# A spectral convolution and a box filter on one core: one DMA fewer per row on SyncE, and seven row additions moved from GpSimd to VectorE

## The chip, the core and the metric

The kernel runs on one NeuronCore of one Trainium2 chip. The metric is the device time of one launch, in microseconds (us). Every engine follows an instruction stream of its own: TensorE (PE in the profile, PEld for its weight loads), VectorE (DVE), ScalarE (ACT), GpSimd (POOL), and SyncE (SP), which here only issues DMA transfers. They meet at semaphores.

## The reference, cut to what matters

The input x is 8 images of 16 channels, 512 x 512, float32. Two layers follow each other, each with a residual:

```python
# _gn: group norm, 8 groups of two channels, over rows and columns
# layer 0
X = rfftn(_gn(x), axes=(-2, -1)); Xr, Xi = real(X), imag(X)
Yr = rconv(Xr, wr) - rconv(Xi, wi) + b_real      # 3x3 convolutions over the spectrum, 16 -> 16 channels
Yi = rconv(Xr, wi) + rconv(Xi, wr) + b_imag
x = x + irfftn(Yr + 1j * Yi)
# layer 1: mean over a 15 x 15 window, zero padding
x = x + mean_filter(_gn(x), 15)
```

## The kernel before

**No transform is computed.** A 3x3 convolution over a spectrum is, back in the image, a sum of products of the image with slow waves. Layer 0 therefore needs, for each image row, the normalised row, its Hilbert transform along the width, and channel mixing by matrices that depend on the row (base, cosine and sine terms), and a few border ("wrap", "virtual") terms.

**Layout.** The 512 image rows are split into 8 bands of T = 64 rows. A partition holds one channel of one band, so "row t" below is 128 partitions x 512 columns, and an image has 64 of them. The image stays in SBUF (`img`).

**Layer 0, one row** (`layer0` on each engine, `slot` functions). The work is a chain over the engines:
- ScalarE normalises the row into a high float16 part and a float32 copy (`normalise`, L773 and L774); GpSimd subtracts the two for the low part (`split_g`, L1303).
- SyncE turns the row by two DMA transposes (`turn`, L396) into one of two buffers `xT`, after it has waited for the split (L391) and for the Hilbert product of the row two before (L394).
- TensorE multiplies it with the Hilbert matrix (`front_hilbert`, L472, 12 matmuls), ScalarE and VectorE split the product in two parts (L781, L1121), and TensorE mixes channels (`mix`, L562, with the wrap terms at L569, 10 steps of four matmuls in quadrants) into the banks p0, p1, p2. TensorE's order is: Hilbert product of row t+1, then mixing of row t. The late half of a row's p0 terms is done in the mixing of the next row, which then counts `p0_ready`.
- VectorE multiplies p1 and p2 with the waves (`wave_terms`, L1163 and L1169), GpSimd adds these and the image row (`add_terms`, L1310 and L1313), VectorE adds p0 and takes statistics (`finish_row`, L1178 and L1181), ScalarE adds a half mean (L790, L800) and counts the row in `x1_whole`.
- From the third step of a mixing on, TensorE waits until VectorE is through with the p1 and p2 of the row before (L630, L631).

**The matrices.** A row's twelve block matrices (high and low parts of six) are built once in setup by VectorE (L1001), stored to a DRAM tensor `bd_dram` (L376), and fetched for every row of every image into one of RB = 4 slots of `bd_all` (`fetch`, L385). The wrap matrix of a row comes from a table in DRAM into `wrap_mat` (L386). Slot t % 4 is free when row t-4 has been mixed. SyncE's queue is strictly in order; its order is written out in `matrices`: turn row t, wait for row t-4, fetch row t.

**Sums for layer 1.** The box filter needs the sum of rows 0 to 7 (`head`) and of rows 57 to 63 (`tail`). Both are running additions by GpSimd (`presum`, L1324 and L1327), a row at a time, in the slot five rows after the row; `presummed` counts the two finished sums, and ScalarE (L870) and VectorE (L1238) wait for both before layer 1. To hold these additions, GpSimd's first 16 slots are written out, and its loop covers the rest.

**Layer 1** turns rows on TensorE, sums them with a band matrix and stores them; VectorE, ScalarE and GpSimd split and subtract rows, while ScalarE's queue loads the next image. An image is one turn of a hardware loop on every engine; the last image is written out after the loop.

**Setup.** SyncE's queue carries, in this order: 19 tables (L334), the weights and biases (L339 to L344), the first image (L348), and later the matrices' stores. VectorE's long chain begins at L929, when the last weight load has landed.

Of the kernel before, what the change touches and what calls it, by code (L numbers as in the profile page):

```python
# [32 lines left out]
F16 = mybir.dt.float16  # L33
ALU = mybir.AluOpType
ACT = mybir.ActivationFunctionType

P = 128
B, C, H, W = 8, 16, 512, 512
HB = P // C
HL = HB // 2  # L40
# [28 lines left out]
GROUP_T = 4  # L69
REC = 12 * HP  # L70
WRAP_SCALE = 4096.0
# [85 lines left out]
def build(nc, x, w_real, w_imag, b_real, b_imag, tab, bd_dram, out):  # L157
    x_v = x.rearrange("b c (s hl t) w -> b s c hl (t w)", s=2, hl=HL)
    out_v = out.rearrange("b c (s hl t) w -> b s c hl (t w)", s=2, hl=HL)
    with ExitStack() as ctx:  # L160
# [30 lines left out]
        stage = [ob_all[:, s * 3 * W:(s + 1) * 3 * W].bitcast(F16) for s in range(2)]  # L191
        assert GROUP_T * REC <= 6 * W
        vbase, vrow, vterm = q_row[0], q_row[1], term_row[0]
        hv = [sb(f"hv{l}", [NV, 2, HZ], F16) for l in range(2)]
        bd_all = sb("bd_all", [P, RB, REC], F16)
        bd = [bd_all[:, s].rearrange("p (j m) -> p j m", j=12) for s in range(RB)]
        flat_bd = bd_all[:].rearrange("p s r -> p (s r)").bitcast(F32)
# [7 lines left out]
        xT = [row.bitcast(F16).rearrange("p (k m) -> p k m", k=8) for row in (piece[9], xT_more[:])]  # L205
        wrap_mat = [sb(f"wrap_mat{s}", [P, P], F16) for s in range(RB)]
        wrap_row = sb("wrap_row", [P, W], F16)
# [45 lines left out]
        vg_split, vh_split, uv_kept, vz_split = sem("vg_split"), sem("vh_split"), sem("uv_kept"), sem("vz_split")  # L253
        bd_made = sem("bd_made")
        bd_stored = [sem(f"bd_stored{s}") for s in range(2)]
        bd_in = [sem(f"bd_in{s}") for s in range(RB)]
# [74 lines left out]
        def _(sp):  # L331
            for n in TABLES:
                if n not in IN_DRAM:
                    sp.dma_start(tb[n][:], tab[n]).then_inc(tab_in, 16)  # L334
            sp.wait_ge(zeroed, 1)
            for i, wr in enumerate((w_real, w_imag)):
# [37 lines left out]
            for g in range(T // GROUP_T):  # L374
                sp.wait_ge(bd_made, g + 1)
                sp.dma_start(bd_dram[g * GROUP_T:(g + 1) * GROUP_T].rearrange("t p r -> p t r"),  # L376
                             stage[g % 2][:, 0:GROUP_T * REC].rearrange("p (t r) -> p t r", t=GROUP_T)
                             ).then_inc(bd_stored[g % 2], 16)
            for s in range(2):
                sp.wait_ge(bd_stored[s], 8 * (T // GROUP_T))  # L380
            sp.dma_start(tail, tab["hilbert_kernel"]).then_inc(bias_in, 16)

            def matrices(b):
                def fetch(t, s):
                    sp.dma_start(bd_all[:, s], bd_dram[t]).then_inc(bd_in[s], 16)  # L385
                    sp.dma_start(wrap_mat[s][:], tab["wrap_h16"][t]).then_inc(bd_in[s], 16)  # L386

                def turn(t, s, first):

                    sp.wait_ge(g_split, b * T + t + (PRIMED + 1))  # L390
                    sp.sem_inc(split_seen, 1)  # L391
                    if first * NG + s >= 2:
                        sp.wait_ge(h_made, b * T + t + (PRIMED - 1))
                        sp.sem_inc(slot_seen, 1)  # L394
                    for i in range(2):
                        sp.dma_start_transpose(xT[s % 2][:, :, (1 - i) * HP:(2 - i) * HP],  # L396
                                               gp_flat[s][i * HP:(i + 1) * HP]).then_inc(xt_in[s % 2], 16)

                sp.wait_ge(uv_summed, PRIMED + (b + 1) * NCH)
                for t in range(RB):  # L400
                    fetch(t, t)
                for t in range(NG):
                    turn(t, t, 0)
                    if t >= RB:
                        sp.wait_ge(p0_ready, b * T + (PRIMED + t - RB + 1))
                        fetch(t, t % RB)
                with sp.Fori(1, T // NG) as i:
                    for s in range(NG):
                        turn(i * NG + s, s, 1)
                        sp.wait_ge(p0_ready, b * T + i * NG + (PRIMED + s - RB + 1))  # L410
                        fetch(i * NG + s, s % RB)

# [18 lines left out]
        def _(pe):  # L431
# [99 lines left out]
            def layer0(b):  # L531
# [53 lines left out]
                def mix(i, s, first):  # L585
# [34 lines left out]

                    pe.wait_ge(bd_in[s % RB], 32 * (b * (T // RB) + i * (NG // RB) + s // RB + 1))
                    pe.wait_ge(h_split, PRIMED + n + 1)
# [285 lines left out]
        def _(dve):  # L908
# [88 lines left out]
            for g in range(T // GROUP_T):  # L997
                if g >= 2:
                    dve.wait_ge(bd_stored[g % 2], 16 * (g // 2))
                rows = slice(g * GROUP_T, (g + 1) * GROUP_T)  # L1000
                V.tensor_tensor(stage[g % 2][:, 0:GROUP_T * REC].rearrange("p (q c h) -> p q c h", c=C, h=HL),  # L1001
                                smat[:, rows].rearrange("p t j o -> p (t j) o").unsqueeze(3)
                                .broadcast_to([P, 12 * GROUP_T, C, HL]),
                                tb["hl_mask16"][:].unsqueeze(1).unsqueeze(1).broadcast_to([P, 12 * GROUP_T, C, HL]),
                                ALU.mult).then_inc(bd_made, 1)
                for t in itertools.islice(rest, 3):
                    count_row(0, t)
# [82 lines left out]
            def layer0(b):  # L1090
# [92 lines left out]
                def slot(i, s, first):  # L1183
# [6 lines left out]
                    if t + 1 < T:  # L1190
                        low_hilbert(n + 1, (s + 1) % NG)

                slot(0, 0, 0)
                virtual_means()
# [4 lines left out]
                for s in range(NG):  # L1199
                    slot(1, s, 1)  # L1200
                with dve.Fori(2, T // NG - 1) as i:
                    for s in range(NG):
                        slot(i, s, 2)
# [68 lines left out]
        def _(pool):  # L1272
# [26 lines left out]
            def layer0(b):  # L1299
# [15 lines left out]
                def presum(n, t):  # L1315

                    total, links = (head, head_chain) if t <= R else (tail, tail_chain)
                    at_r, start = (t, 0) if t <= R else (t - (T - R), T - R)
                    pool.wait_ge(x1_whole, n + 1)
                    if at_r == 0:  # L1320
                        return
                    rows = R if t <= R else R - 1
                    if at_r == 1:
                        ins = G.tensor_tensor(total, img[:, start, :], img[:, t, :], ALU.add)  # L1324
                    else:
                        pool.wait_ge(links, b * (rows - 1) + at_r - 1)
                        ins = G.tensor_tensor(total, total, img[:, t, :], ALU.add)  # L1327
                    ins.then_inc(links if at_r < rows else presummed, 1)

# [12 lines left out]
                for t in range(1, 3):  # L1342
                    split_g(b * T + t, t)
                for t in range(R + 9):
                    slot(t // NG, t % NG, t // NG, sum_t=t - 5 if 5 <= t <= R + 5 else None)
                assert (R + 9) % NG == 0
                with pool.Fori((R + 9) // NG, T // NG - 1) as i:
                    for s in range(NG):
                        slot(i, s, 2)
                for t in range(T - NG, T):  # L1350
# [54 lines left out]
```

## Time and profile before

| | |
|---|---|
| median of 3 runs | 3860.23 us (3859.74 to 3861.21) |
| the profiled execution's own time | 3868.96 us |
| its span, first to last instruction | 3867.2 us |
| granted TensorE clock, mean | 0.961 |
| busy: TensorE / VectorE / GpSimd / ScalarE | 3360.8 / 3155.5 / 2632.0 / 2109.3 us |
| one image, both layers, about | 463 us, of it 262 us from the first to the last Hilbert product of layer 0 |

Times inside the profile are microseconds from the span's start. A line such as "L562" is a line of the kernel. The chain of waits is followed back from the last instruction, at each step to what released it. "Idle before" is time that the engine stood still ahead of an instruction, with the one that ended it. A large busy share does not make an engine the bound: what counts is which wait ends last in a stage.

### The profile page before, as it was taken

How to read it: one execution, taken by the hardware profiler on the slowest of the kernel's cores; microseconds unless marked ns; L12 is line 12 of the kernel's file. 1: busy time of each engine (PE TensorE's matmuls, PEld its weight loads, DVE VectorE, ACT ScalarE, POOL GpSimd, SP SyncE). 2: the span in 40 equal slices, each digit the busy share in tenths (PEclk: the TensorE clock that was granted, in tenths of full speed). 3: DMA queues.
4: the chain of work that ended last, by engine and by line, in shares of the span. 5: the costliest groups of instructions: out<-in, count | busy, mean ns of one | idle time of the engine just before them, and what ended most of it. 6: DMA issues, size and time to landing. Idle time of an engine off the chain costs nothing.

```text
span 3867.2 us, 115816 instructions
## 1 busy us (share of the span) xinstructions
PE 3360.8 (87%) x38496; PEld 2224.2 (58%) x38496; DVE 3155.5 (82%) x5870; ACT 2109.3 (55%) x4286; POOL 2632.0 (68%) x2177
## 2 busy tenths in 40 slices
PE   2189889997999979899798998999899998999978
PEld 1055576555765557555675556755476555765557
DVE  7888877887778878788787887888877887888976
ACT  0068733786337852578426873278633785247842
POOL 5079853997539966499546985389853996639954
PEclk8599999999999999999999999999999999999999
DMA  6556567554766538655485554755467653865634
GB/s 158 180 100 121 104 176 196 110 121 80 221 170 117 120 83 245 144 118 121 116 235 113 121 118 139 223 108 121 96 185 192 113 121 76 232 162 118 123 79 137
DMA packets 785608, 542.37 MB, mean 140 GB/s; under 512 B 655216, under 2 KB 730576, under 8 KB 772944
## 3 DMA queue, kind: packets, MB, share of 16 engines
q1 hardware_dynamic: 762832, 420.23, 47.9%
q10 hardware_dynamic: 22400, 117.46, 11.6%
q8 instruction: 195, 3.19, 0.4%
q14 instruction: 181, 1.48, 0.1%
HBM read 256.31 MB, written 146.80 MB: 104 GB/s over the span
## 4 chain that ended last, share of the span: by engine, by line
SPq 39%; PE 31%; issue 11%; DVE 11%; ACT 3%; POOL 3%; DMA 2%; ACTq 1%; DVEq 0%; POOLq 0%
SPq L396 27%; PE h_ps L674 14%; PE p L700 6%; SPq L385 5%; PE p L511 4%; SPq L386 4%; DVE ob_all L1235 2%; PE p L562 2%; ACT arena L743 2%; PE p L480 1%; DVE ob_all L1001 1%; ACTq L883 1%; DVE stat L990 1%; PE h_ps L472 1%; DMA xT_more<-arena 1%
## 5 line engine op out<-in xcount | busy, mean ns | idle before, releaser
L562 PE MATMUL p<-arena,bd_all 64*64 64x512 f16 x16896 | 1278.8, 380 | 25.6 <-DVE ob_all L1169 23.7
L1362 POOL TENSOR_TENSOR arena<-img 128x512 f32<-128x512 f32 x392 | 498.7, 1273 | 461.8 <-PE h_ps L674 439.8
L1310 POOL TENSOR_TENSOR ob_all<-ob_all,img 128x512 f32<-128x512 f32 x512 | 662.6, 1294 | 176.2 <-DVE ob_all L1163 169.4
L743 ACT ACTIVATE arena<-h_ps 128x512 f16<-128x512 f32 x512 | 305.7, 597 | 838.2 <-PE h_ps L674 595.0
L562 PEld LDWEIGHTS p<-arena,bd_all 64*64 64x64 f16 x16896 | 562.9, 105 | 347.5 <-issue 139.4
L1313 POOL TENSOR_TENSOR ob_all<-ob_all 128x512 f32<-128x512 f32 x512 | 653.0, 1275 | 40.2
L1163 DVE SCALAR_TENSOR_TENSOR ob_all<-p,bias_c,cosw 128x256 f32<-128x256 f32 x1024 | 448.1, 479 | 167.6 <-PE p L562 138.7
L674 PE MATMUL h_ps<-bd_all,arena 128*128 128x128 f32 x3584 | 539.6, 286 | 0.0
L1219 DVE TENSOR_TENSOR arena<-h_ps,arena 128x512 f16<-128x512 f32 x512 | 353.2, 690 | 207.9 <-ACT arena L743 206.3
L674 PEld LDWEIGHTS h_ps<-bd_all,arena 128*128 128x128 f32 x3584 | 447.6, 191 | 121.2 <-issue 114.7
L800 ACT ACTIVATE img<-img,half_row (+1 forms) x1024 | 484.9, 527 | 4.8
L773 ACT ACTIVATE arena<-img,sc 128x512 f16 (+1 forms) x512 | 432.0, 844 | 32.3 <-POOL arena L1303 31.3
L1169 DVE SCALAR_TENSOR_TENSOR ob_all<-p,bias_c,cosw 128x256 f32<-128x256 f32 x1024 | 443.6, 475 | 0.0
L472 PE MATMUL h_ps<-hilbert,arena 128*128 128x256 f16 x3072 | 379.6, 273 | 63.9 <-DMA arena<-arena 59.3
L472 PE MATMUL h_odd<-hilbert,xT_more 128*128 128x256 f16 x3072 | 380.2, 274 | 58.4 <-DMA xT_more<-arena 45.6
L1303 POOL TENSOR_TENSOR arena<-arena 128x512 f16<-128x512 f32 x256 | 296.9, 1160 | 193.5 <-ACT arena L774 193.5
L472 PEld LDWEIGHTS h_odd<-hilbert,xT_more 128*128 128x128 f16 x3072 | 280.1, 98 | 208.1 <-DMA xT_more<-arena 126.2
L472 PEld LDWEIGHTS h_ps<-hilbert,arena 128*128 128x128 f16 x3072 | 280.0, 98 | 208.1 <-DMA arena<-arena 115.9
L1181 DVE BATCH_NORM_STATS2 stat<-img (+1 forms) x512 | 355.5, 694 | 51.8
L700 PE MATMUL p<-band,arena 128*128 128x135 f16 (+1 forms) x4096 | 332.5, 225 | 58.1 <-DVE ob_all L1235 56.2
L511 PE MATMUL p<-img,bd_all 128*64 128x256 f32 x2048 | 306.5, 406 | 76.0 <-POOL bd_all L1282 49.9
L1235 DVE SCALAR_TENSOR_TENSOR ob_all<-p,img 128x512 f32<-128x512 f32 x512 | 348.7, 681 | 5.1 <-PE p L700 4.3
(166 smaller groups left out, 4992.8 us busy)
## 6 DMA issues: line engine op xcount, KB each, us to landing
out<-ob_all SPq DMA_DIRECT2D x512, 256.0 KB, 4.2
bd_all<-bd_dram SPq DMA_DIRECT2D x512, 192.0 KB, 2.3
img<-in_x ACTq DMA_DIRECT2D x168, 512.0 KB, 7.0
img<-in_x ACTq DMA_DIRECT2D x112, 256.0 KB, 4.9
wrap_mat<-tab_wrap_h SPq DMA_DIRECT2D x512, 32.0 KB, 2.0
img<-in_x SPq DMA_DIRECT2D x24, 512.0 KB, 23.7
bd_dram<-ob_all SPq DMA_DIRECT2D x16, 768.0 KB, 3.5
arena<-arena SPq DMA_TRANSPOSE x512, 2.7
```

Of the source, the lines that this page charges most:

```text
L396: sp.dma_start_transpose(xT[s % 2][:, :, (1 - i) * HP:(2 - i) * HP], gp_flat[s][i * HP:(i + 1) * HP]).then_inc(xt_in[s % 2], 16)
L472: m = mm(dst(a), row[:, 4 * lx + k, :], tb["hilbert16"][:, lt, k, 0:cols], start=(half == 0 and i == 0), stop=(half == 1 and i == 2))
L511: m = mm(uv_ps[i * HP:(i + 1) * HP, cols], w, img[:, 2 * q + i, cols], start=(q == 0 and part == 0), stop=(q == T // 2 - 1 and part == 1), ...
L562: m = mm(bank[out_half * HP:(out_half + 1) * HP, :], bd[s % RB][rows, 6 * lm + (j if own else j + 1), :], part, start=opens and i3 == 0, s ...
L674: m = mm(turned_ps[u % 2][:, k, :], row[:, k * P:(k + 1) * P], mat, start=(i == 0), stop=(i == len(terms) - 1))
L700: m = mm(p0[0][:, lo:hi], parts[u % 2][:, l, k, :], tb["band16"][:, lo - k * P + R:hi - k * P + R], start=(u == 0 and k == 0 and l == 0), ...
L800: ins = nc.scalar.activation(row, row, ACT.Identity, bias=half_row[:, s, a:a + 1])
L1163: ins = V.scalar_tensor_tensor(t1[:, a, :], p1[:, a * HALF:(a + 1) * HALF], bias_c[:, 1, t, 1 - a:2 - a], cosw[:, a, :], ALU.subtract, ALU ...
L1169: ins = V.scalar_tensor_tensor(t2[:, a, :], p2[:, a * HALF:(a + 1) * HALF], bias_c[:, 0, t, 1 - a:2 - a], sinw[:, a, :], ALU.add, ALU.mult)
L1310: G.tensor_tensor(q, term_row[s % 2][0], parity(img[:, t, :]), ALU.add).then_inc(first_added, 1)
L1313: G.tensor_tensor(q, q, term_row[s % 2][1], ALU.add).then_inc(q_done, 1)
L1362: G.tensor_tensor(diff[u % 2], img[:, u + R, :], img[:, u - R - 1, :], ALU.subtract).then_inc(moved, 1)
```

## The change

1. The record of a row in `bd_dram` and `bd_all` grows by 128 elements per partition, which hold the wrap matrix. A DMA from DRAM to DRAM writes the table into the records once, in setup, ahead of the weight loads. The separate fetch L386 is gone, `bd_in` counts 16 per row in place of 32.
2. SyncE's order in layer 0 is: turn row t, wait for row t-5, fetch row t-1; the last row's fetch follows the loop.
3. The head sum (rows 0 to 7) is made by VectorE, behind its other work in slots 9 to 15, instead of GpSimd in slots 6 to 12; GpSimd keeps the tail sum, and its loop begins at row 8.

```diff
-REC = 12 * HP
+REC = 12 * HP + P
...
+        STAGED = 12 * HP
...
-        bd = [bd_all[:, s].rearrange("p (j m) -> p j m", j=12) for s in range(RB)]
+        bd = [bd_all[:, s, 0:STAGED].rearrange("p (j m) -> p j m", j=12) for s in range(RB)]
+        wrap_mat = [bd_all[:, s, STAGED:REC] for s in range(RB)]
...
-        wrap_mat = [sb(f"wrap_mat{s}", [P, P], F16) for s in range(RB)]
...
                     sp.dma_start(tb[n][:], tab[n]).then_inc(tab_in, 16)
+            sp.dma_start(bd_dram[:, :, STAGED:REC], tab["wrap_h16"]).then_inc(wrap_stored, 16)
             sp.wait_ge(zeroed, 1)
...
+            sp.wait_ge(wrap_stored, 16)
             sp.dma_start(tail, tab["hilbert_kernel"]).then_inc(bias_in, 16)
...
                     sp.dma_start(bd_all[:, s], bd_dram[t]).then_inc(bd_in[s], 16)
-                    sp.dma_start(wrap_mat[s][:], tab["wrap_h16"][t]).then_inc(bd_in[s], 16)
...
                 for t in range(NG):
                     turn(t, t, 0)
-                    if t >= RB:
-                        sp.wait_ge(p0_ready, b * T + (PRIMED + t - RB + 1))
-                        fetch(t, t % RB)
+                    if t > RB:
+                        sp.wait_ge(p0_ready, b * T + (PRIMED + t - RB))
+                        fetch(t - 1, (t - 1) % RB)
                 with sp.Fori(1, T // NG) as i:
                     for s in range(NG):
                         turn(i * NG + s, s, 1)
-                        sp.wait_ge(p0_ready, b * T + i * NG + (PRIMED + s - RB + 1))
-                        fetch(i * NG + s, s % RB)
+                        sp.wait_ge(p0_ready, b * T + i * NG + (PRIMED + s - RB))
+                        fetch(i * NG + s - 1, (s - 1) % RB)
+                sp.wait_ge(p0_ready, (b + 1) * T + (PRIMED - RB))
+                fetch(T - 1, (T - 1) % RB)
...
-                    pe.wait_ge(bd_in[s % RB], 32 * (b * (T // RB) + i * (NG // RB) + s // RB + 1))
+                    pe.wait_ge(bd_in[s % RB], 16 * (b * (T // RB) + i * (NG // RB) + s // RB + 1))
...
+                def sum_head(t):
+
+                    dve.wait_ge(x1_whole, b * T + t + 1)
+                    if t == 1:
+                        ins = V.tensor_tensor(head, img[:, 0, :], img[:, 1, :], ALU.add)
+                    else:
+                        dve.wait_ge(head_chain, b * (R - 1) + t - 1)
+                        ins = V.tensor_tensor(head, head, img[:, t, :], ALU.add)
+                    ins.then_inc(head_chain if t < R else presummed, 1)
...
                 for s in range(NG):
                     slot(1, s, 1)
+                    if s > 0:
+                        sum_head(s)
...
-                for t in range(R + 9):
-                    slot(t // NG, t % NG, t // NG, sum_t=t - 5 if 5 <= t <= R + 5 else None)
-                assert (R + 9) % NG == 0
-                with pool.Fori((R + 9) // NG, T // NG - 1) as i:
+                for s in range(NG):
+                    slot(0, s, 0)
+                with pool.Fori(1, T // NG - 1) as i:
                     for s in range(NG):
-                        slot(i, s, 2)
+                        slot(i, s, 1)
```

GpSimd's `presum` keeps only its branch for the tail.

## Rows read from the trace of the kernel before

**Rows 1.** The page of the kernel before: busy shares, queue q1, chain by line, one DMA issue

```profile
PE 3360.8 (87%) x38496; PEld 2224.2 (58%) x38496; DVE 3155.5 (82%) x5870; ACT 2109.3 (55%) x4286; POOL 2632.0 (68%) x2177
...
q1 hardware_dynamic: 762832, 420.23, 47.9%
...
SPq L396 27%; PE h_ps L674 14%; PE p L700 6%; SPq L385 5%; PE p L511 4%; SPq L386 4%; DVE ob_all L1235 2%; PE p L562 2%; ACT arena L743 2%; PE p L480 1%; DVE ob_all L1001 1%; ACTq L883 1%; DVE stat L990 1%; PE h_ps L472 1%; DMA xT_more<-arena 1%
...
bd_all<-bd_dram SPq DMA_DIRECT2D x512, 192.0 KB, 2.3
```

**Rows 2.** SyncE's queue in the steady part of layer 0: start us, us, what

```profile
2197.66 2.52 SPq L396 DMA_TRANSPOSE arena<-arena  x2
2200.37 0.43 SPq L385 DMA_DIRECT2D bd_all<-bd_dram  x1
2200.98 0.33 SPq L386 DMA_DIRECT2D wrap_mat<-tab_wrap_h  x1
2201.65 2.52 SPq L396 DMA_TRANSPOSE xT_more<-arena  x2
```

**Rows 3.** TensorE's timeline: first and ninth Hilbert product, fifth image, then the last

```profile
2173.05 1.48 PE L472 MATMUL h_odd<-hilbert,xT_more 128*128 128x256 f16 x12
...
2205.67 1.48 PE L472 MATMUL h_odd<-hilbert,xT_more 128*128 128x256 f16 x12
...
3548.28 1.48 PE L472 MATMUL h_ps<-hilbert,arena 128*128 128x256 f16 x12 [0.62 <-DMA arena<-arena]
...
3580.27 1.48 PE L472 MATMUL h_ps<-hilbert,arena 128*128 128x256 f16 x12 [0.59 <-DMA arena<-arena]
```

**Rows 4.** TensorE's timeline, fifth image: the Hilbert products of rows 7, 8 and 16

```profile
2088.53 1.48 PE L472 MATMUL h_odd<-hilbert,xT_more 128*128 128x256 f16 x12
...
2092.36 1.48 PE L472 MATMUL h_ps<-hilbert,arena 128*128 128x256 f16 x12
...
2128.57 1.48 PE L472 MATMUL h_ps<-hilbert,arena 128*128 128x256 f16 x12 [0.85 <-DMA arena<-arena]
```

**Rows 5.** Busy us by window: PE, PEld, DVE, ACT, POOL; clock; DMA share; GB/s

```profile
2173.21:2238.38 65.17, 62.23 (x834) 35.78 (x833) 57.65 (x113) 52.78 (x113) 59.00 (x49) 1.00 0.59 121
```

**Rows 6.** VectorE's timeline, rows at TensorE's pace

```profile
2084.58 0.88 DVE L1163 SCALAR_TENSOR_TENSOR ob_all<-p,bias_c,cosw 128x256 f32<-128x256 f32 x2 [0.19 <-PE p L562]
```

**Rows 7.** Timeline of VectorE and GpSimd in one steady row

```profile
2202.70 1.30 POOL L1310 TENSOR_TENSOR ob_all<-ob_all,img 128x512 f32<-128x512 f32 x1 [0.22 <-DVE ob_all L1163]
...
2204.07 1.28 POOL L1313 TENSOR_TENSOR ob_all<-ob_all 128x512 f32<-128x512 f32 x1
...
2204.71 0.67 DVE L1121 SCALAR_TENSOR_TENSOR arena<-h_ps,arena 128x512 f16<-128x512 f32 x1
...
2205.31 1.16 POOL L1303 TENSOR_TENSOR arena<-g_more,arena 128x512 f16<-128x512 f32 x1
```

**Rows 8.** Who waited for whom, the last rows of the second image's layer 0

```profile
PE h_ps L472 <- DMA arena<-arena: 2.5, 2, 1.4
...
PE h_odd L472 <- DMA xT_more<-arena: 1.1, 1, 1.1
```

**Rows 9.** One line, GpSimd's L1327: durations ns min/median/max, first and last start

```profile
L1327 POOL TENSOR_TENSOR arena<-arena,img x88: 1259/1272/1292, 244.6 to 3724.2; 128x512 f32<-128x512 f32 x88
```

**Rows 10.** One line, VectorE's L1114: durations ns min/median/max, first and last start

```profile
L1114 DVE TENSOR_TENSOR ob_all<-ob_all x8: 691/692/692, 207.5 to 3447.2; 128x512 f32<-128x512 f32 x8
```

**Rows 11.** Timeline of setup, VectorE and GpSimd

```profile
24.11 1.23 DVE L320 TENSOR_TENSOR img<-img,trig_h 128x1024 f32<-128x1024 f32 x1
...
31.88 3.33 POOL L321 TENSOR_TENSOR img<-img 128x1024 f32<-128x1024 f32 x1
...
33.03 3.26 DVE L320 TENSOR_TENSOR img<-img,trig_swapped 128x1024 f32<-128x1024 f32 x1
```

**Rows 12.** The start of setup: timeline, then busy time by window (columns as in rows 5)

```profile
17.94 0.45 DVE L929 TENSOR_REDUCE sc<-img 128x1 f32<-128x288 f32 x1 [15.21 <-DMA sc<-in_L_conv_b_imag]
...
8.00:10.00 2.00, 0.00 (x0) 0.00 (x0) 0.00 (x0) 0.00 (x0) 0.00 (x0) 1.00 0.87 259
```

More of the change, by code:

```diff
@@ L191, in build @@
         stage = [ob_all[:, s * 3 * W:(s + 1) * 3 * W].bitcast(F16) for s in range(2)]
-        assert GROUP_T * REC <= 6 * W
+        STAGED = 12 * HP
+        assert GROUP_T * STAGED <= 6 * W
         vbase, vrow, vterm = q_row[0], q_row[1], term_row[0]
@@ L254, in build @@
         bd_made = sem("bd_made")
+        wrap_stored = sem("wrap_stored")
         bd_stored = [sem(f"bd_stored{s}") for s in range(2)]
@@ L375, in _ @@
                 sp.wait_ge(bd_made, g + 1)
-                sp.dma_start(bd_dram[g * GROUP_T:(g + 1) * GROUP_T].rearrange("t p r -> p t r"),
-                             stage[g % 2][:, 0:GROUP_T * REC].rearrange("p (t r) -> p t r", t=GROUP_T)
+                sp.dma_start(bd_dram[g * GROUP_T:(g + 1) * GROUP_T, :, 0:STAGED].rearrange("t p r -> p t r"),
+                             stage[g % 2][:, 0:GROUP_T * STAGED].rearrange("p (t r) -> p t r", t=GROUP_T)
                              ).then_inc(bd_stored[g % 2], 16)
@@ L1000, in _ @@
                 rows = slice(g * GROUP_T, (g + 1) * GROUP_T)
-                V.tensor_tensor(stage[g % 2][:, 0:GROUP_T * REC].rearrange("p (q c h) -> p q c h", c=C, h=HL),
+                V.tensor_tensor(stage[g % 2][:, 0:GROUP_T * STAGED].rearrange("p (q c h) -> p q c h", c=C, h=HL),
                                 smat[:, rows].rearrange("p t j o -> p (t j) o").unsqueeze(3)
@@ L1315, in presum @@
                 def presum(n, t):
-                    total, links = (head, head_chain) if t <= R else (tail, tail_chain)
-                    at_r, start = (t, 0) if t <= R else (t - (T - R), T - R)
+                    at_r, rows = t - (T - R), R - 1
                     pool.wait_ge(x1_whole, n + 1)
@@ L1321, in presum @@
                         return
-                    rows = R if t <= R else R - 1
                     if at_r == 1:
-                        ins = G.tensor_tensor(total, img[:, start, :], img[:, t, :], ALU.add)
+                        ins = G.tensor_tensor(tail, img[:, T - R, :], img[:, t, :], ALU.add)
                     else:
-                        pool.wait_ge(links, b * (rows - 1) + at_r - 1)
-                        ins = G.tensor_tensor(total, total, img[:, t, :], ALU.add)
-                    ins.then_inc(links if at_r < rows else presummed, 1)
+                        pool.wait_ge(tail_chain, b * (rows - 1) + at_r - 1)
+                        ins = G.tensor_tensor(tail, tail, img[:, t, :], ALU.add)
+                    ins.then_inc(tail_chain if at_r < rows else presummed, 1)
                 def slot(i, s, first, sum_t=None):
```

## The prediction, made before the changed kernel ran

> **What bounds the kernel now.** I read the page first, for the shares of the engines and the chain that ended last, then SyncE's queue, then TensorE, VectorE and GpSimd row by row. TensorE is busy for 87% of the span, yet the chain names SyncE's L396 (the transposes) for 27%, L385 and L386 (the two matrix fetches) for 5 and 4% [rows 1]. So the busiest engine is often not the one that sets the end.
>
> In the steady part of layer 0 SyncE never rests. A row costs it two transposes (2.52 us), the fetch of the block matrices (0.37 to 0.43 us), the fetch of the wrap matrix (0.33 us) and the small moves and waits around them; transposes start at 2197.66 and 2201.65, 4.0 us apart [rows 2]. What L386 costs with its address moves lies between the end of L385 (2200.80) and its own end (2201.31): 0.51 us, and about 0.04 of issue behind it: 0.55 us. TensorE follows: eight rows take 2205.67 - 2173.05 = 32.6 us, 4.08 us a row; in the last image they take 3580.27 - 3548.28 = 32.0 us [rows 3]. Early in an image, while the transposes still have a lead, TensorE sets its own pace: from 2088.53 to 2092.36 is 3.83 us, and that pace repeats for two to eight rows per image until the lead is used up [rows 4]. Its granted clock is 1.00 in the steady part, the 2.4 GHz level [rows 5], so the slower pace there is not the clock's.
>
> VectorE works through a row in this order: L1163, L1169, L1178, L1181, L1121. In those rows of 3.83 us it waits 0.19 for TensorE ahead of L1163: it needs about 3.66 [rows 6]. GpSimd needs L1303, L1310 and L1313, which is 1.16 + 1.30 + 1.28 = 3.74 us, 3.71 with their small overlaps [rows 7]. So below SyncE's 4.08 lie TensorE at 3.83, GpSimd at 3.71, VectorE at 3.66.
>
> **The parts, in the order of their size.**
>
> *One fetch fewer per row on SyncE, and the new order.* The 128 wrap elements ride in the same record, so L386 goes: 0.55 us from each row of about 4.05, leaving 3.5, under TensorE's 3.83. The record grows from 192 to 224 KB; its issue costs the same 0.37 to 0.43, since that time does not follow bytes: a 32 KB fetch takes 0.33. TensorE is then the bound. I do not take 3.83 x 8 = 30.6 us for eight rows but 31.0, as each engine also turns a loop and three of them lie within 0.2 us. That is 1.6 us per eight rows; about 40 rows (16 to 56) run at SyncE's pace: 5 x 1.6 = 8.0 us an image, seven images 56, the last one 5 x 1.0 = 5: **-61 us**. Bounds: 30.6 gives -76; 31.8 gives -30.
> The changed order costs nothing by itself. Turning row t may start once row t-2's Hilbert product is made, and the fetch of t-1 follows it 2.5 us later; it asks for the matrices' slot of row t-5, which is free a whole row before. It lands some 2.3 us after issue [rows 1], about 5.3 us after that Hilbert product. Row t-1's mixing starts about 7.7 us after it: two rows of TensorE (a mixing and a Hilbert product each). Even 2 us late it would not show. What it gives is lead: in the old order turn, then wait for row t-4, then fetch, made SyncE finish just as it could start the next.
>
> *The tail of layer 0.* The last rows carry pitches up to 5.3 us: TensorE waits there 2.5 and 1.1 us in three places for a transposed row that landed late [rows 8]. With SyncE ahead by up to 2 us I let half of these 3.6 go: 1.8 x 8 = **-14 us** (bounds 0 and -29).
>
> *The head sum.* GpSimd loses seven additions of 1.27 us in rows 1 to 7; with them its row takes 3.71 + 1.27 = 4.98 us [rows 9], and it is the bound: nine pitches of TensorE take 2128.57 - 2088.53 = 40.0 us [rows 4]. VectorE gets seven additions in its slots 9 to 15. The nearest row is L1114, the same form (two float32 inputs in SBUF, 512 elements), 0.69 us with GpSimd idle [rows 10]. It goes behind L1121, ahead of the next L1163, which releases both GpSimd (L1310) and TensorE's third step of the next mix. No wait is added that is not long met. VectorE has 0.17 us of room, so it becomes the bound for seven rows.
> What they cost depends on GpSimd. In setup both engines work from SBUF: VectorE's L320 took 1.23 us alone (24.11) and 3.26 us when it was issued at 33.03, into GpSimd's L321 that ran until 35.21; it ended 1.08 us after that [rows 11]. So such an addition waits for the running GpSimd instruction, then runs. In the steady row L1121 ends at about 2205.38, just when L1313 ends (2205.35) and L1303 begins (2205.31) [rows 7]. If the addition gets in between, the row is 3.66 + 0.08 + 0.69 = 4.43 us; if L1303 is first, 3.70 + 1.13 + 0.67 = 5.5. It is a tie; I take the mean, 4.97. Nine pitches: 2 x 3.83 + 7 x 4.97 = 42.4 against 40.0: 2.4 x 8 = **+19 us** (bounds 38.7 and 46.2: -11 and +49).
> The Trainium skill ("SBUF — State Buffer", section "Who interferes with whom") says that a VectorE instruction with two SBUF inputs excludes a GpSimd instruction that reads SBUF, and that the one issued first holds the ports until it ends. The setup rows agree; without that rule these rows would take 4.35 us and the term would be -15 us.
>
> *Setup.* A copy from DRAM to DRAM is put on SyncE's queue ahead of the weight loads: 64 x 128 pieces of 256 bytes, 2.1 MB. VectorE starts its chain only when the last of those loads has landed (L929 at 17.94 after 15.2 us idle), and stays on the chain for the rest of setup, so a delay goes straight to the end [rows 12]. No row shows such a copy. From below: 2.1 MB at the 259 GB/s of the tables' load are 8 us [rows 12]. From above: queue q1 spent 47.9% of 16 x 3867 us on 762,832 packets, 39 ns each [rows 1]; 8192 of them on 16 engines take 20 us, and 40 if both sides are paid. The tables are in at about 13 us, the copy ends at 21 to 53, the loads land some 1.8 us later: delay +5 to +37. I take 15 us of copy: **+12 us**.
>
> Sum: -61 - 14 + 19 + 12 = -44 us. The profiled execution took 3868.96 us (span 3867.2), so 3825 for its like; the median of the runs is 8.7 us lower, which I carry over unchanged: 3860.23 - 44 = **3816 us**.
>
> **Rivals.**
> *The addition slips in between each time* (or there is no exclusion). For it: an instruction that already waits is served at the hand-over, as at 35.21; once in, it delays L1303 and with it GpSimd's phase, which favours the next one. -61 - 14 - 11 + 12 = -74: 3786 us. Chance 0.22.
> *It loses to L1303 each time.* For it: two waits are looked at before it starts, and GpSimd idles until L1163, so the phase repeats. -61 - 14 + 49 + 12 = -14: 3846 us. Chance 0.15.
> *Slower: the DMA side, not SyncE, sets the pace of the transposes.* If the 2.52 us of a pair are the queue's back-pressure, they stretch by what L386 leaves, the steady part stays at 32.6, TensorE's wait moves from the issue to the landing, and the sum is -14 + 19 + 12 = +17: 3877 us. It decides if the issue stretches beyond 3.83 - 0.95 = 2.9 us for a pair. Against it: the DMA engines are 0.59 busy in that stretch [rows 5]. Chance 0.08.
> *The copy is far slower than its bounds.* From 64 us of delay the kernel is slower, which needs 130 ns a packet; at 80 us it gives 3884. Chance 0.04.
> My forecast keeps 0.45; 0.06 is left for what I do not see.
>
> **The numbers.** Forecast 3816 us. Range 3778 to 3858: down to the first rival with a setup of +5 (3779), up to the second with +24 (3858); its ends leave out the slower cases and half of the unseen. About 0.2% (8 us) is what a measurement of this kernel can tell from no change. Faster by more than that: the forecast, the first two rivals but for a slow copy: 0.81. Within it: the second rival with a copy of over 20 us, and some of the unseen: 0.08. Slower: 0.11.
>
> **What would show it.** Right: no L386; transposes start 3.8 to 3.9 us apart with SyncE waiting for the Hilbert product (L394) between them; eight steady rows of TensorE in 31 us; no GpSimd addition at t below 57; L929 at about 30 us. VectorE's additions are on average 1.2 us long as recorded, with GpSimd idle ahead of L1310. Wrong: pairs of transposes longer than 2.52 us; steady rows above 32 us; L929 after 55 us; additions of 0.69 us (first rival) or of 1.8 us (second).

## The result: 3745.35 us, ratio 0.970

| | before | after |
|---|---|---|
| median (lowest to highest) | 3860.72 (3859.74 to 3864.39), 4 runs | 3745.35 (3743.27 to 3746.3), 4 runs |
| ratio, 95% interval | | 0.9699 [0.9682, 0.9716] |
| span of the profiled execution | 3867.2 | 3744.4 |
| its own time | 3868.96 | 3746.19 |

The change saves 3%: 115 us by the medians, and 122.8 us between the two profiled spans, from which the stages below are read. I had forecast 44 us. The page of the kernel after, the parts that answer to [rows 1] (busy shares, queue q1, the chain by engine and by line; a line number of after is 5 above that of before for TensorE and for VectorE in layer 0, 17 above for GpSimd's L1303, L1310 and L1313 and for VectorE's L1235; SyncE's L385, L394 and L396 are now L389, L397 and L399; L567 is the mixing, L477 the Hilbert product, L679 and L705 are layer 1):

```profile
PE 3342.5 (89%) x38496; PEld 2211.3 (59%) x38496; DVE 3183.2 (85%) x5926; ACT 2111.4 (56%) x4286; POOL 2595.3 (69%) x2121
...
q1 hardware_dynamic: 697312, 422.30, 48.9%
...
PE 78%; DVE 11%; issue 4%; ACT 2%; DMA 2%; POOL 1%; SPq 1%; ACTq 1%; DVEq 0%; POOLq 0%
PE p L567 25%; PE h_ps L679 14%; PE h_ps L477 9%; PE h_odd L477 9%; PE p L705 6%; PE p L516 4%; PE p L574 3%; PE h_ps L567 2%; DVE stat L995 2%; DVE ob_all L1252 2%; PE p L485 1%; ACT arena L748 1%; DVE ob_all L1006 1%; PE h_ps L574 1%; ACTq L888 1%
```

SyncE has left the chain: 1% in place of the 27 + 5 + 4% that L396, L385 and L386 held. TensorE carries 78% of it, at the same number of matmuls.

SyncE's queue in the steady part (start, us), the counterpart of [rows 2]:

```profile
2100.93 2.52 SPq L399 DMA_TRANSPOSE xT_more<-arena  x2
2103.64 0.43 SPq L389 DMA_DIRECT2D bd_all<-bd_dram  x1
2104.76 2.53 SPq L399 DMA_TRANSPOSE arena<-arena  x2
```

Whom SyncE waited for in the 140 us from 2070 on (total us, times, longest):

```profile
SPq L397 <- PE h_odd L477: 5.6, 18, 0.4
SPq L397 <- PE h_ps L477: 4.6, 14, 0.4
```

A pair of transposes still takes 2.52 us, the fetch 0.43, and now SyncE waits for the Hilbert product in 32 of some 36 rows (10.2 us in all). It is ahead.

TensorE's timeline, the first and the ninth Hilbert product in that stretch, to hold against [rows 3]:

```profile
2080.12 1.48 PE L477 MATMUL h_ps<-hilbert,arena 128*128 128x256 f16 x12
...
2110.87 1.48 PE L477 MATMUL h_ps<-hilbert,arena 128*128 128x256 f16 x12
```

And a window's busy times (us, PE, PEld, DVE, ACT, POOL, clock, DMA share, GB/s), against [rows 5]:

```profile
2086.02:2147.55 61.53, 61.53 (x837) 35.38 (x833) 57.69 (x113) 52.98 (x114) 59.18 (x49) 1.00 0.61 127
```

Eight rows take 30.75 us against 32.6, and TensorE is busy for 61.53 of 61.53 us. The granted clock is 1.00 as before.

**Where the time went.** The start of every Hilbert product in TensorE's timeline cuts an image into stages. Means over the eight images, in us (row 0 to row 7, and so on):

| stage | before | after | x 8 |
|---|---|---|---|
| rows 0 to 7 | 28.67 | 28.65 | 0 |
| rows 7 to 18, with the head sum | 48.21 | 44.74 | -27.8 |
| rows 18 to 56, steady | 154.66 | 146.02 | -69.1 |
| rows 56 to 63, tail | 30.64 | 26.88 | -30.1 |
| launch to the first Hilbert product | 207.4 | 217.0 | +9.6 |
| from one image to the next (7 times) | 200.36 | 199.71 | -4.6 |
| after the last one | 159.8 | 159.1 | -0.7 |

The sum is -123, the difference of the spans.

Setup first, the timeline of SyncE's issues and of VectorE's first instruction that needs the weights, beside [rows 12]:

```profile
9.73 0.68 SPq L337 DMA_DIRECT2D bd_dram<-tab_wrap_h  x1
10.46 10.70 SPq L342 DMA_DIRECT2D img<-in_L_conv_w_real  x2
...
28.07 0.45 DVE L934 TENSOR_REDUCE sc<-img 128x1 f32<-128x288 f32 x1 [25.34 <-DMA sc<-in_L_conv_b_imag]
```

And a window inside the copy (columns as above):

```profile
14.00:16.00 2.00, 0.00 (x0) 0.00 (x0) 0.00 (x0) 0.00 (x0) 0.00 (x0) 1.00 1.22 278
```

L934 starts at 28.07 in place of 17.94: the copy cost 10.1 us.

Then seven rows of VectorE and GpSimd with a head addition (L1205, after L1126). One of them, with the next row's L1168:

```profile
2047.52 0.86 DVE L1168 SCALAR_TENSOR_TENSOR ob_all<-p,bias_c,cosw 128x256 f32<-128x256 f32 x2
...
2050.01 1.28 POOL L1330 TENSOR_TENSOR ob_all<-ob_all 128x512 f32<-128x512 f32 x1
2050.47 0.68 DVE L1126 SCALAR_TENSOR_TENSOR arena<-h_ps,arena 128x512 f16<-128x512 f32 x1
2051.06 0.78 DVE L1205 TENSOR_TENSOR arena<-arena,img 128x512 f32<-128x512 f32 x1
2051.24 1.62 POOL L1320 TENSOR_TENSOR arena<-g_more,arena 128x512 f16<-128x512 f32 x1
2051.76 0.86 DVE L1168 SCALAR_TENSOR_TENSOR ob_all<-p,bias_c,cosw 128x256 f32<-128x256 f32 x2
```

The addition is issued at 2051.06 while GpSimd's L1330 still has 0.23 us to go, and takes the turn: GpSimd's L1320, 1.16 us otherwise [rows 7], is recorded with 1.62. The row is 4.24 us (2047.52 to 2051.76) and VectorE stands still nowhere in it. That repeats in all seven rows of all images. The line view has six of the seven (durations in ns: least, median, most); the first addition, which reads two image rows, is a line of its own, eight times 704 to 716 ns:

```profile
L1205 DVE TENSOR_TENSOR arena<-arena,img x48: 704/774/789, 264.8 to 3407.9; 128x512 f32<-128x512 f32 x48
```

The tail's rows stand at 3.83 us, and no wait of a Hilbert product for a transposed row is left in the last rows ([rows 8] had 3.6 us of them in one image).

### The profile page after: what moved, and what is told of

It reads as the page before. It is cut to its first block, busy times and chain, and to the rows that moved or that the text cites. A ratio compares the mean times of both kernels' runs of the same rounds, so it can differ in the third digit from the quotient of the medians.

```text
span 3744.4 us, 114575 instructions
## 1 busy us (share of the span) xinstructions
PE 3342.5 (89%) x38496; PEld 2211.3 (59%) x38496; DVE 3183.2 (85%) x5926; ACT 2111.4 (56%) x4286; POOL 2595.3 (69%) x2121
## 4 chain that ended last, share of the span: by engine, by line
PE 78%; DVE 11%; issue 4%; ACT 2%; DMA 2%; POOL 1%; SPq 1%; ACTq 1%; DVEq 0%; POOLq 0%
PE p L567 25%; PE h_ps L679 14%; PE h_ps L477 9%; PE h_odd L477 9%; PE p L705 6%; PE p L516 4%; PE p L574 3%; PE h_ps L567 2%; DVE stat L995 2%; DVE ob_all L1252 2%; PE p L485 1%; ACT arena L748 1%; DVE ob_all L1006 1%; PE h_ps L574 1%; ACTq L888 1%
## 5 line engine op out<-in xcount | busy, mean ns | idle before, releaser
L567 PE MATMUL p<-arena,bd_all 64*64 64x512 f16 x16896 | 1291.3, 381 | 33.4 <-DVE ob_all L1174 23.1
L567 PEld LDWEIGHTS p<-arena,bd_all 64*64 64x64 f16 x16896 | 552.2, 105 | 380.2 <-issue 239.3
L1327 POOL TENSOR_TENSOR ob_all<-ob_all,img 128x512 f32<-128x512 f32 x512 | 664.2, 1297 | 86.3 <-DVE ob_all L1168 59.6
L1330 POOL TENSOR_TENSOR ob_all<-ob_all 128x512 f32<-128x512 f32 x512 | 654.1, 1278 | 40.1
L679 PE MATMUL h_ps<-bd_all,arena 128*128 128x128 f32 x3584 | 539.5, 286 | 0.0
L679 PEld LDWEIGHTS h_ps<-bd_all,arena 128*128 128x128 f32 x3584 | 447.6, 191 | 121.2 <-issue 115.4
L1168 DVE SCALAR_TENSOR_TENSOR ob_all<-p,bias_c,cosw 128x256 f32<-128x256 f32 x1024 | 447.5, 478 | 57.1 <-PE p L567 19.8
L1320 POOL TENSOR_TENSOR arena<-arena 128x512 f16<-128x512 f32 x256 | 308.5, 1205 | 192.6 <-ACT arena L779 192.6
L705 PE MATMUL p<-band,arena 128*128 128x135 f16 (+1 forms) x4096 | 332.4, 224 | 57.7 <-DVE ob_all L1252 55.7
L477 PE MATMUL h_ps<-hilbert,arena 128*128 128x256 f16 x3072 | 379.8, 273 | 0.4 <-DMA arena<-arena 0.3
L477 PE MATMUL h_odd<-hilbert,xT_more 128*128 128x256 f16 x3072 | 379.8, 273 | 0.0
L477 PEld LDWEIGHTS h_odd<-hilbert,xT_more 128*128 128x128 f16 x3072 | 280.2, 98 | 135.8 <-issue 99.2
L477 PEld LDWEIGHTS h_ps<-hilbert,arena 128*128 128x128 f16 x3072 | 280.3, 98 | 131.8 <-issue 94.2
L1320 POOL TENSOR_TENSOR arena<-g_more,arena 128x512 f16<-128x512 f32 x256 | 311.8, 1218 | 65.5 <-ACT g_more L779 45.5
```

The lines of the kernel that those rows point to most:

```text
L477: m = mm(dst(a), row[:, 4 * lx + k, :], tb["hilbert16"][:, lt, k, 0:cols], start=(half == 0 and i == 0), stop=(half == 1 and i == 2))
L567: m = mm(bank[out_half * HP:(out_half + 1) * HP, :], bd[s % RB][rows, 6 * lm + (j if own else j + 1), :], part, start=opens and i3 == 0, s ...
L679: m = mm(turned_ps[u % 2][:, k, :], row[:, k * P:(k + 1) * P], mat, start=(i == 0), stop=(i == len(terms) - 1))
L705: m = mm(p0[0][:, lo:hi], parts[u % 2][:, l, k, :], tb["band16"][:, lo - k * P + R:hi - k * P + R], start=(u == 0 and k == 0 and l == 0), ...
L1168: ins = V.scalar_tensor_tensor(t1[:, a, :], p1[:, a * HALF:(a + 1) * HALF], bias_c[:, 1, t, 1 - a:2 - a], cosw[:, a, :], ALU.subtract, ALU ...
L1320: G.tensor_tensor(gp[s][:, 1, :], g32[s % 2], gp[s][:, 0, :], ALU.subtract).then_inc(g_split, 1)
```

## The experiments

Each experiment was given a theory and a rival before it ran. Theory A, from the two traces: SyncE's time to issue was the bound; the fetch that went carries the steady part and the tail; the new order gives nothing; the head sum gives a part of its own, because the additions fall on the hand-over between two GpSimd instructions. The rivals are in the expectations. The stages named below are those of the table; "tail" is rows 56 to 63.

**1. The second fetch put back** (new order and head sum stay, no copy):

```diff
                     sp.dma_start(bd_all[:, s], bd_dram[t]).then_inc(bd_in[s], 16)
+                    sp.dma_start(wrap_mat[s], tab["wrap_h16"][t]).then_inc(bd_in[s], 16)
```

> The changed kernel, but with the wrap matrix fetched by itself again (in the new order, no copy in setup). Theory A (SyncE's time per row is what bound the kernel before, and the new order alone gives nothing): SyncE needs 4.05 us a row again, the 38 steady rows (18 to 56) of an image go back from 146.0 to about 154.7 us, the tail (rows 56 to 63) from 26.9 to 30 or so; 8 x (8.7 + 3.5 + 1) = +105, -10 for the copy in setup: about 3840 us. Theory B (the lead that the new order gives is what hides late transpositions, and the second fetch only rides along): the tail stays at 27, the steady part below 150 us, total below 3790 us.

Measured: 3859.56 us, 0.999 [0.998, 1.0] of before. Steady rows 154.3 us, tail 30.7, rows 7 to 18 47.5. Theory B falls: with two issues the lead of the new order hides nothing. The loss is 20 us larger than theory A said, for the head's rows also fall back by 2.8 us an image: at SyncE's pace most of the additions' gain is lost.

**2. The old order with one fetch:**

```diff
...
-                        sp.wait_ge(p0_ready, b * T + i * NG + (PRIMED + s - RB))
-                        fetch(i * NG + s - 1, (s - 1) % RB)
+                        sp.wait_ge(p0_ready, b * T + i * NG + (PRIMED + s - RB + 1))
+                        fetch(i * NG + s, s % RB)
```

> The changed kernel with SyncE's order of before: turn row t, wait for row t-4, fetch row t. Theory A: with one fetch SyncE needs 3.5 us a row against TensorE's 3.83, and the wait for row t-4 ends about when the pair of transposes has been issued: 3745 to 3750 us, steady rows at 3.84 us, tail 26.9. Theory B (the lead counts): the tail's excess of 3.8 us an image comes back and part of the steady part's, 3775 us or more.

Measured: 3749.6 us, 0.971 [0.9694, 0.9726]; stages 28.66, 44.77, 146.05, 26.82 us, the changed kernel's to 0.06. The order is worth nothing here. SyncE has the same time to spare either way: between rows 18 and 56 it waits 11.4 us an image in this run and in the changed kernel (waits over 0.15 us), and never in the kernel before or in experiment 1.

**3. The head sum back on GpSimd:**

```diff
-                    if s > 0:
-                        sum_head(s)
...
+                    slot(t // NG, t % NG, t // NG, sum_t=t - 5 if 5 <= t <= R + 5 else None)
```

> The changed kernel with the head sum on GpSimd as before. Theory A (GpSimd bound seven rows at 4.96 us before, VectorE now needs 4.25 for them): rows 7 to 18 go from 44.7 to 48 or 49 us, 8 x 3.5 to 4.3 = +28 to +34: about 3776 us. Rival (the excess of before in these rows came from SyncE, and GpSimd's additions hide under its lead): rows 7 to 18 stay below 46 us, 3755 us or less.

Measured: 3775.82 us, 0.9774 [0.9758, 0.9791]. Rows 7 to 18 take 48.2 us, as before the change, though SyncE is no longer a bound. So GpSimd's additions are enough by themselves to make these rows that long, and the rival falls. The head sum on VectorE is worth 3.5 us an image there.

**4. Only the head sum moved, on the kernel before:**

> The kernel before with nothing but the head sum moved to VectorE (two fetches, old order, no copy). Theory A: SyncE's 4.05 us a row hides most of the additions (VectorE needs 4.25 in seven rows), rows 7 to 18 fall from 48.2 to about 45.5, the rest stays: -20 to -25, about 3838 us. Rival (gains of the parts need each other; the additions come on top of SyncE's pace): no gain, 3855 us or more.

Measured: 3856.0 us, 0.9983 [0.9973, 0.9994]; rows 7 to 18 47.3 us (-0.9 an image), steady 154.7, tail 30.4. The gain is a third of what I expected: with GpSimd out of the way SyncE's 4.05 us and its late transpositions take the place of the bound, and TensorE waits 4.1 us an image for transposed rows in this stage. The part needs the other one. By the bare time the rival (3855 or more) is met; against the kernel before of the same session, 3863.9 us, there is a small gain, 7.9 us. This kernel and that of experiment 1 differ in SyncE's order alone, and stand at 0.9983 and 0.999: with two fetches the order is worth nothing either.

**5. Only the fetch merged, on the kernel before** (old order, GpSimd's head sum):

> The kernel before with nothing but the wrap matrix in the fetched record (old order, head sum on GpSimd, copy in setup). Theory A (the one fetch fewer carries the steady part and the tail by itself, and the head sum on VectorE is worth 30 us on top): 3776 to 3782 us, steady rows 18 to 56 at 146 us, tail 27. Rival (order and fetch need each other when GpSimd holds the splits back): steady part or tail above 148 and 28 us, 3790 or more.

Measured: 3774.69 us, 0.978 [0.9765, 0.9795]; stages 28.65, 48.35, 146.04, 27.06. One fetch fewer is worth 85 us by itself, the copy paid, and brings both the steady part and the tail.

**6. A tiny second DMA.** Issue time or bytes and packets?

```diff
                     sp.dma_start(bd_all[:, s], bd_dram[t]).then_inc(bd_in[s], 16)
+                    sp.dma_start(dummy[s][0:1], tab["wrap_h16"][t][0:1]).then_inc(bd_in[s], 16)
...
-                    pe.wait_ge(bd_in[s % RB], 16 * (b * (T // RB) + i * (NG // RB) + s // RB + 1))
+                    pe.wait_ge(bd_in[s % RB], 32 * (b * (T // RB) + i * (NG // RB) + s // RB + 1))
```

> The changed kernel plus, behind each row's fetch, a second DMA of 256 bytes to one partition that nobody reads (TensorE waits for its landing as it did for the wrap matrix). Theory A (what bound the kernel before is SyncE's time to issue, whatever a DMA carries): SyncE needs 4.0 us a row again, steady rows 18 to 56 at about 154 us in place of 146, the tail's late transpositions come back, 3745 + 8 x 12 = about 3840 to 3850 us. Theory B (the 128 small packets a row on the DMA engines were what slowed the transpositions and landings; that the issue is short counts little): 3745 to 3760 us, steady rows at 3.84 us.

Measured: 3827.93 us, 0.9905 [0.9888, 0.9922]. SyncE's queue in the steady part:

```profile
2192.56 2.52 SPq L401 DMA_TRANSPOSE arena<-arena  x2
2195.35 0.37 SPq L390 DMA_DIRECT2D bd_all<-bd_dram  x1
2195.90 0.25 SPq L391 DMA_DIRECT2D dummy<-tab_wrap_h  x1
2196.50 2.52 SPq L401 DMA_TRANSPOSE xT_more<-arena  x2
```

The chain by engine, from this run's page:

```profile
SPq 40%; PE 32%; DVE 11%; issue 10%; ACT 3%; DMA 2%; POOL 1%; ACTq 1%; DVEq 0%; POOLq 0%
```

256 bytes a row bring SyncE back to a pitch of 3.94 us and 40% of the chain, steady rows to 151.8 us and the tail to 29.7. Between rows 18 and 56 SyncE again never waits. The time is 12 us short of theory A's least, 3840. The issue costs 0.25 us against 0.33 for the real fetch; 38 rows x 0.08 = 3.0 us, and its steady part is 2.5 us under that of experiment 1. Theory B falls: what bound the kernel is that SyncE issues, and what it moves counts only through those 0.08 us. One path is not told apart from the others here: TensorE also waits for the landing of this second DMA, 0.9 us an image between rows 18 and 56. The tail returns with it (experiments 1, 4 and 6 have two issues and 29.7 to 30.7 us, all others one and 26.8 to 27.1): late transpositions reach TensorE only while SyncE has no time to spare.

**7. The additions one instruction earlier**, ahead of L1126, in the middle of GpSimd's second addition:

```diff
                         finish_row(n - 2, i * NG + s - 2, (s - 2) % NG, first - (s < 2))
+                    if sum_t > 0:
+                        sum_head(sum_t)
                     if t + 1 < T:
                         low_hilbert(n + 1, (s + 1) % NG)
...
-                    slot(1, s, 1)
-                    if s > 0:
-                        sum_head(s)
+                    slot(1, s, 1, s)
```

> The changed kernel with VectorE's seven additions one instruction earlier, ahead of the split of the Hilbert product instead of behind it, so that they are issued while GpSimd's second addition of add_terms runs. Theory A (exclusive use of the ports, and the changed kernel's place happens to be the hand-over between two GpSimd instructions): an addition is recorded with 1.3 to 1.5 us, its row takes 4.8 to 5.0 us in place of 4.25, 8 x 7 x 0.6 = +25 to +40: 3770 to 3785 us. Rival (VectorE's addition and GpSimd share the ports and the place does not matter): additions of 0.7 us, 3745 us within 5.

Measured: 3780.62 us, 0.9778 [0.9761, 0.9794]; rows 7 to 18 49.1 us. Its timeline in one row:

```profile
2071.23 1.28 POOL L1330 TENSOR_TENSOR ob_all<-ob_all 128x512 f32<-128x512 f32 x1
2071.69 1.37 DVE L1195 TENSOR_TENSOR arena<-arena,img 128x512 f32<-128x512 f32 x1
2072.47 1.61 POOL L1320 TENSOR_TENSOR arena<-g_more,arena 128x512 f16<-128x512 f32 x1
```

And the addition's line (durations in ns, least, median, most):

```profile
L1195 DVE TENSOR_TENSOR arena<-arena,img x48: 1296/1367/1376, 263.7 to 3440.1; 128x512 f32<-128x512 f32 x48
```

The addition issued at 2071.69 ends at 2073.06, 0.55 us after GpSimd's L1330 ends (2072.51): it waits for the rest of that instruction, then runs, and L1320 waits for it in turn. This row takes 4.85 us. The same seven additions cost 35 us more for standing 0.6 us earlier. This is the exclusion that the Trainium skill states ("SBUF — State Buffer", section "Who interferes with whom"), and the trace agrees: all 56 additions end 0.55 us after the end of the GpSimd instruction that ran when they were issued, here and in the changed kernel, although they are issued about 0.82 us ahead of that end here and 0.23 us there. The measurement adds who follows: the engine already waiting, each time. That VectorE is simply preferred would look the same in these rows; the rows from setup in the last section speak against it.

**8. The copy on ScalarE's queue**, after `setup_done`:

```diff
-            sp.dma_start(bd_dram[:, :, STAGED:REC], tab["wrap_h16"]).then_inc(wrap_stored, 16)
...
             act.wait_ge(setup_done, 1)
+            act.dma_start(bd_dram[:, :, STAGED:REC], tab["wrap_h16"]).then_inc(wrap_stored, 16)
```

> The changed kernel with the copy of the wrap matrices on ScalarE's DMA queue, after setup_done, while the DMA engines are under half busy, instead of ahead of the weight loads. Theory A (the copy's whole cost is the 10 us by which it holds the weight loads back): VectorE's chain starts at 17.9 us again, 3735 us. Rival (it collides with the matrices' stores, which VectorE waits for): less than 5 us gained.

Measured: 3742.67 us, 0.9686 [0.9669, 0.9702]; the first Hilbert product starts at 209.8 us in place of 217.0 (207.4 before the change). VectorE's chain starts at 17.93 again, so theory A holds for the weights, but part of it comes back as the rival says: VectorE's wait for the first store of the matrices grows (13.5 us here and 14.9 in experiment 11, with the copy there; 11.4 to 12.4 in the runs without it). First the timeline of this run, then that of the kernel before:

```profile
95.35 0.68 ACTq L754 DMA_DIRECT2D bd_dram<-tab_wrap_h  x1
...
118.92 3.36 DVE L1006 TENSOR_TENSOR ob_all<-arena,hl_mask 128x3072 f16<-128x3072 f16 x1 [13.51 <-DMA bd_dram<-ob_all]
```

```profile
117.23 3.36 DVE L1001 TENSOR_TENSOR ob_all<-arena,hl_mask 128x3072 f16<-128x3072 f16 x1 [11.89 <-DMA bd_dram<-ob_all]
```

7.2 us are gained in setup. By the whole time it cannot be told from the changed kernel: the intervals overlap.

**9. The additions spread** over slots 6, 9, 12, 15, 17, 20 and 23:

```diff
...
+                sum_at = {6: 1, 9: 2, 12: 3, 15: 4, 17: 5, 20: 6, 23: 7}
+                for t in range(2, 3 * NG):
+                    slot(t // NG, t % NG, t // NG)
+                    if t in sum_at:
+                        sum_head(sum_at[t])
+                with dve.Fori(3, T // NG - 1) as i:
...
```

> The changed kernel with VectorE's seven additions spread over slots 6, 9, 12, 15, 17, 20 and 23 (one more turn of its loop written out), not in seven slots on end. Theory A (VectorE has about 0.29 us of room a row, which one addition of 0.7 every third row fits in): rows 7 to 18 fall from 44.7 to 42.3 us, the rest grows by under 0.5, 8 x 2 = -16: about 3729 us. Rival (an addition always reaches TensorE, since VectorE is late for the third step of the next mixing, whatever room follows): each costs the same 0.4 us wherever it stands, 3743 to 3748 us.

Measured: 3743.72 us, 0.9688 [0.9672, 0.9704]; layer 0 245.5 us an image in place of 246.3. Neither is right: the seven rows with an addition take 4.02 to 4.23 us, 0.27 above 3.83 on average, where in seven rows on end each costs 0.37 (2.6 us over 11 x 3.83). VectorE's room of a row, the 0.18 us that it waits ahead of L1168 in the rows between, takes up only part of an addition; the rest reaches TensorE at once, in its third step. A row without and one with an addition (of the next, L1168 no longer waits):

```profile
2066.07 0.88 DVE L1168 SCALAR_TENSOR_TENSOR ob_all<-p,bias_c,cosw 128x256 f32<-128x256 f32 x2 [0.18 <-POOL ob_all L1329]
...
2069.62 0.78 DVE L1205 TENSOR_TENSOR arena<-arena,img 128x512 f32<-128x512 f32 x1
...
2070.32 0.86 DVE L1168 SCALAR_TENSOR_TENSOR ob_all<-p,bias_c,cosw 128x256 f32<-128x256 f32 x2
```

**10 to 12. On one chip: the changed kernel again, 8 and 9 together (11), and additions cut into halves of 256 columns on top of that (12).**

> The changed kernel itself, on the chip of the next three. 0.970 of the kernel before: 3745 to 3750 us.

Measured: 3748.18 us (3742.25 to 3751.23), 0.971 [0.9696, 0.9723].

> The changed kernel with both the additions spread over seven slots three apart and the copy on ScalarE's queue. If the two gains add: layer 0 at 245.4 us an image, first Hilbert product at 210 us, span 3732 us, time 3738, 0.2% under the changed kernel on the same chip. If they do not: within 3 us of it.

Measured: 3735.33 us (3734.64 to 3741.51), 0.9679 [0.9666, 0.9692]; layer 0 245.5 us an image, first Hilbert product at 209.9. The two gains add, as far as 13 us can be told here.

```diff
...
-                    ins = V.tensor_tensor(head, head, img[:, t, :], ALU.add)
+                    t, cols = k // 2 + 1, slice(k % 2 * HALF, (k % 2 + 1) * HALF)
+                    first = img[:, 0, cols] if t == 1 else head[:, cols]
+                    ins = V.tensor_tensor(head[:, cols], first, img[:, t, cols], ALU.add)
...
```

> As the kernel with spread additions and the copy on ScalarE's queue, but each addition cut into two halves of 256 columns, 14 in all, one a slot and every fourth slot free. Theory A (an addition reaches TensorE with what it exceeds VectorE's room and TensorE's slack of some 0.4 us a row together): a half costs 0.35 to 0.5 us and is hidden, rows 7 to 56 take 188.3 us in place of 189.9, 8 x 1.5 = -12 against the whole additions: 3728 us. Rival (a half too waits for the hand-over, about 0.2 us, and pays its start twice): 14 x 0.15 us an image, no better than whole ones, 3738 us or more.

Measured: 3731.97 us (3727.92 to 3737.82), 0.9669 [0.9656, 0.9683], but layer 0 takes 245.7 us an image, no less than with whole additions: rows 7 to 56 take 190.15 against 189.96. The reason is in the addition's line:

```profile
L1206 DVE TENSOR_TENSOR arena<-arena,img x96: 415/504/535, 250.1 to 3424.6; 128x256 f32<-128x256 f32 x96
```

Two halves are 1.0 us where one whole is 0.77: each waits for GpSimd's hand-over by itself (a half is issued 0.22 us before GpSimd's running instruction ends and ends 0.28 us after it; a whole one 0.22 and 0.55). The theory of a hidden half falls; the 3 us by the whole time lie inside the spread of the runs. Both versions beat the changed kernel on the same chip, by 13 and 16 us (0.34 and 0.43%).

## Why the prediction was wrong, point by point

The direction was right, and that SyncE's fetch carries the most of it; the size was not: 3816 us with 3778 as the lower end, 3745 measured. By the terms of the sum (-44 forecast, -123 between the spans):

- **The head sum, +19 us forecast, -28 measured: the step that failed, 47 of the 79 us.** I had called the moment at which L1121 (now L1126) ends "a tie" between the addition and GpSimd's L1303 and taken the mean of winning (4.43 us a row) and losing (5.5). There is no tie: an engine that already waits is served first (experiment 7, and all 56 additions within 0.704 to 0.789 us), and the addition always waits, as it is issued 0.16 to 0.24 us before L1330 ends. The row of 5.5 us never came. The row that came was 4.24, not 4.43: I had added 0.08 us of waiting and taken VectorE's need as 3.66. In rows that VectorE sets, its five instructions start 0.79, 0.79, 0.77, 0.61 and 0.59 us after each other, 3.55 in all. And I set seven dear rows into a window, rows 7 to 16, in which only five fall: the additions in slots 9 to 15 lengthen the steps from Hilbert product 11 to 18. The first rival (3786) had the mechanism right, and I gave it 0.22; its own -11 missed for these two slips.
- **The tail, -14 forecast, -30 measured.** "I let half of these 3.6 go" was a guess between bounds of 0 and -29. All of it went, and a little more: the excess was not only the three waits for a transposed row but the whole of the rows above 3.83. Experiments 1, 4 and 6 against 2, 3 and 5 show that it hangs on SyncE's second issue and on nothing else.
- **The steady part, -61 forecast, -69 measured.** The mechanism held to the row: SyncE's 0.55 us went, TensorE became the bound. I had allowed 0.4 us in eight rows for loops and for three engines near each other; the row takes 3.84 us in all places. The lower bound, 30.6 us for eight rows, was the right one (30.75), over 38 rows at 32.6 us for eight before. What I did not see is that these 32.6 us were seven rows of 3.9 to 4.1 us and one of 4.5, at the turn of SyncE's loop, where its pairs of transposes start 4.39 us apart (2217.82 to 2222.21). SyncE's time to spare now covers this turn as well.
- **Setup, +12 forecast, +10 measured.** Right in size, by two errors that offset each other. I had the copy run for 15 us and the loads land 1.8 us after it. It ran for about 8, my bound from below: the DMA share is 1.05 to 1.27 from 12 to 20 us and 0.29 in the next two. But the other weight loads were issued only behind it, up to 26.69 us, and L934 could start only some 7.5 us after its end: what the copy delayed was SyncE's queue, as the row of 10.70 us shows.
- **The order, 0 forecast.** Right (experiment 2).
- **The slower rivals.** "The DMA side sets the pace": a pair took 2.52 to 2.53 us at the faster pitch too, and experiment 6 shows that bytes do not count. "The copy is far slower": 10 us.
- **Not forecast:** 4.6 us between images (200.36 to 199.71 us, seven times). Other runs of the same layer 1 lie at 198.9 to 200.5, so this may be no effect of the change; it stays open.

The range failed because I let its lower end stop at the first rival with a setup of +5, but kept the tail and the steady part at their likeliest values there, though both had bounds that reached 15 us further down each. Even with these it would have ended at 3749, 4 us above the result; the head sum's own bound, -11, was 17 us too high.

## What to carry to other kernels

A queue that only issues transfers is an engine with a budget per row: count its issues by their time in its own timeline, not by their bytes, and merge small fetches into large ones; once it has time to spare, rows made late by other things vanish as well. When a sum moves to another engine, look at what each engine does at the very moment it will be issued: behind a running instruction that excludes it, standing 0.6 us earlier cost 35 us here. And where a term is a tie between two outcomes, find out who wins from a row in which one already waits, rather than take the mean.

## What the runs showed of the hardware that I had not expected

- VectorE's additions with two SBUF inputs and GpSimd's instructions exclude each other, and the one that waits goes next. Against 0.69 us for the same form with GpSimd idle [rows 10], an addition took 0.08 us longer when 0.23 us of GpSimd's instruction were left and 0.68 us longer when 0.82 were left, 0.14 to 0.15 us less than what was left; GpSimd's next was longer by 0.45 us (1.16 to 1.61) each time. GpSimd's waiting instruction goes ahead of VectorE's next in the same way, as setup of the changed kernel shows:

```profile
43.15 3.25 DVE L322 TENSOR_TENSOR img<-img,trig_swapped 128x1024 f32<-128x1024 f32 x1
...
45.28 1.60 POOL L1299 TENSOR_TENSOR bd_all<-virt_h,c_mask 128x256 f32<-128x256 f32 x1
46.44 1.52 DVE L323 TENSOR_TENSOR img<-img 128x1024 f32<-128x1024 f32 x1
```

  L1299 (0.62 us by its median) waits for the end of L322 at 46.40 and runs ahead of L323, which VectorE has ready at once: L323 is recorded with 1.52 us in place of 1.22 at 35.49.
- A DMA of 256 bytes cost SyncE 0.25 us to issue, one of 32 KB 0.33, one of 192 or 224 KB mostly 0.34 to 0.43.
- The copy of 8192 pieces of 256 bytes was issued in 0.68 us, but the next issue behind it stood for 10.07 of the 10.70 us of its pair: SyncE was held up until the copy was nearly through. While it ran, the window's DMA share stood at 1.22 and its rate at 278 GB/s. From 2.1 MB in about 8 us, a 256-byte piece between DRAM and DRAM cost an engine an estimated 8 x 16 / 8192 = 16 ns, well under the 39 ns a packet that I had taken from above.
